# A gated cross-attention kernel on one core: its opening in another order

## The chip, the core and the metric

The kernel runs on one core of a Trainium2 chip. A core has five engines that work beside each other and wait for each other through semaphores: TensorE (PE, matrix products, with its weight loads shown apart as PEld), VectorE (DVE), ScalarE (ACT), GpSimd (POOL) and SyncE (SP), which here only issues DMAs. Data lie in SBUF; TensorE writes into eight PSUM banks, which VectorE and ScalarE read. The metric is the device time of one execution in microseconds (us), as the median of several runs.

## The reference

Two blocks, each with an attention over a context and a feed-forward part; a residual stream x of 4 x 512 x 128 goes through all four.

```
x = x + tanh(g_xattn[0]) * attention0(layernorm(x), ctx)     # 16 heads of 8, 154 keys
x = x + tanh(g_ffn[0])   * quantised_gated_ffn(layernorm(x)) # 128 -> 384 -> 128
x = x + tanh(g_xattn[1]) * attention1(layernorm(x), ctx)     # the same with a causal mask
x = x + tanh(g_ffn[1])   * scan_ffn(layernorm(x))            # a gated recurrence over the 4 elements
```

An attention is q = xn Wq' + bq, k = ctx Wk' + bk, v = ctx Wv' + bv, then softmax(q k' / sqrt(8)) v per head and a projection with Wo. Of the whole, the text that follows needs the first attention's opening: the layer norm of the batch elements, the keys, the queries and the maxima of the scores.

## The kernel before

The work is staged by batch element. The programs of the engines are written out by hand, each in its own order; `PE_PLAN`, `ACT_PLAN` and `DVE_PLAN` say at which slot of a step (i = -1 to 4, 20 slots each) a piece of an element's work stands. Each engine takes its instructions strictly in this order, so an instruction that waits holds all behind it.

The opening of the first layer runs thus:

- **Loads.** SyncE issues all loads in one go: x of element 0, the context, the key weights, three attention weights, the tail of the context, x of elements 1 to 3, then the weights of the later parts and the masks. ScalarE issues three small ones, `rows` among them.
- **Norm.** VectorE takes the statistics of an element (`norm_stats`, L1358 and L1361). GpSimd makes 1/sqrt(var + eps) (`root`, L641 and L643). Then the element is scaled to `xn`, by VectorE for the elements in `NORM_ON_DVE` (L1376) and by GpSimd for the others (L651 and L658). TensorE turns it into the one bank `misc` (`turn_normed`, L965) and ScalarE copies it to `xnT` (L759).
- **Keys.** Eight products (`keys`, L946) of 128 x 308: four groups of heads, each for elements 0 and 1 (part 0) and for 2 and 3 (part 1). ScalarE makes the high part `kh` of each (L728), VectorE the sum `K4` (L1309).
- **Query.** TensorE projects `xnT` into `misc` (`project_q`, L971), ScalarE writes its high part `qh` (L766), VectorE its low part `ql` from the same bank (L1416), and SyncE sends both by three DMAs into `Q4` (`queries`). `misc` has one user at a time, in the order of `misc_plan`.
- **Diagonal.** `K4` of one element is spread into the cleared tile `Kd` (L1699 and L746 for element 0, GpSimd's L536 for elements 2 and 3).
- **Units.** For element 0, 22 units: TensorE makes the scores of up to three heads for 128 queries into one of three banks (`scores_for_top`, L988), VectorE takes the maximum over the keys (`take_top`, L1425) and so frees the bank. Between the units TensorE has fillers (`fill`, L1121), whose results nobody reads. Behind unit 12 it turns the normed element 2, elsewhere it makes the values (L957) and the third query.
- **Behind it.** The maxima are split (L1436 and L1438), turned (L1002), copied (L778) and sent by DMAs (L462) into `Q4`; then the scores proper (L1020), exponentials (L787) and weighted values (L1052) of element 0 run, with the units of the next element between them.
- **GpSimd** has, beside the roots, a long list: clears of `Kd[0]` and `Q4[1]`; `Kd[1]`, `V4`, `VT` (L668 to L670); behind VectorE's diagonal copies `Q4[2]`, `Kd[2]`, `nil` (L505 to L507); norm of element 2; constants of V (L569 to L581); biases; values (L596 and L600); the low part of the third query; `KT` (L549); the diagonal of element 2 (L536).

## Time and profile before

| | |
|---|---|
| median of 3 runs | 335.45 us (334.67 to 335.69) |
| the profiled execution | 336.59 us, its span 334.6 us |
| TensorE busy | 294.6 us, 88% of the span |
| VectorE busy | 250.6 us, 75% |
| ScalarE busy | 190.9 us, 57% |
| GpSimd busy | 139.9 us, 42% |
| mean granted clock of TensorE | 0.974 of full |

A busy share is an average over the whole program. In the opening, each engine has its own gaps, and only the timelines of that stretch say which of them the next piece of work waits for. A timeline row gives the start of a group of like instructions, how long the group takes, the engine, the line, the operation, the tile written and the tiles read, the count, and in brackets how long the engine had stood idle and what ended that.

### The profile page before, as it was taken

To read this page: it belongs to the slowest core of one execution; us is meant where nothing else is said; L and a number is where in the kernel's file an instruction comes from. 1 tells how busy PE (TensorE), PEld (TensorE's weight loads), DVE (VectorE), ACT (ScalarE), POOL (GpSimd) and SP (SyncE) were. 2 spreads that over 40 slices of the span, in tenths; PEclk is the share of its full clock that TensorE was granted. 3 is DMA by queue.
4 is the path that set the end of the run, shared out by engine and by line. 5 is a ranking of instruction groups with operands and counts; after the bars stand their busy time and mean duration, and the time that the engine had idled before them with its cause. 6 is when DMAs were issued, how large, how long until landed. Compare 5 with 4: busy or idle time off the path is not lost. (4 is left out here: it accounts for less than half of the span.)

```text
span 334.6 us, 4564 instructions
## 1 busy us (share of the span) xinstructions
PE 294.6 (88%) x1456; PEld 169.4 (51%) x1456; DVE 250.6 (75%) x549; ACT 190.9 (57%) x311; POOL 139.9 (42%) x274
## 2 busy tenths in 40 slices
PE   1789899799989798996997879699989998999994
PEld 1458555455533364442545667574755654434462
DVE  5689877888987379999998895686697692442834
ACT  1672276466476744889899415236566557664232
POOL 6669892752050401684002194921386217141100
PEclk9979999999999999998999997879999999999999
DMA  7920100020000000000000102020002000000004
GB/s 214 357 98 34 71 31 11 0 102 10 1 8 3 0 0 2 1 0 1 0 0 2 69 25 95 2 102 0 10 6 101 4 2 9 0 3 0 1 2 125
DMA packets 9688, 12.57 MB, mean 38 GB/s; under 512 B 896, under 2 KB 5376, under 8 KB 9664
## 3 DMA queue, kind: packets, MB, share of 16 engines
q1 hardware_dynamic: 9232, 11.80, 9.9%
q10 hardware_dynamic: 432, 0.47, 0.7%
q8 instruction: 12, 0.20, 0.3%
q14 instruction: 12, 0.10, 0.1%
HBM read 4.27 MB, written 1.05 MB: 16 GB/s over the span
## 5 line engine op out<-in xcount | busy, mean ns | idle before, releaser
L1425 DVE TENSOR_REDUCE sb_nm<-ps_top 128x3 f32<-128x462 f32 (+2 forms) x168 | 97.7, 626 | 28.1 <-PE ps_top L988 17.9
L787 ACT ACTIVATE sb_pr<-ps_score 128x512 f32<-128x512 f32 (+1 forms) x148 | 81.9, 583 | 56.7 <-PE ps_score L1020 47.5
L988 PE MATMUL ps_top<-sb_Kd,sb_Q 128*128 128x462 f32 (+3 forms) x240 | 71.8, 355 | 4.1 <-DVE sb_nm L1425 3.2
L1020 PE MATMUL ps_score<-sb_Q,sb_Kd 128*128 128x512 f32 x119 | 54.7, 470 | 1.4 <-ACT sb_pr L787 1.0
L988 PEld LDWEIGHTS ps_top<-sb_Kd,sb_Q 128*128 128x128 f32 x240 | 45.1, 195 | 15.8 <-DVE sb_nm L1425 10.5
L1020 PEld LDWEIGHTS ps_score<-sb_Q,sb_Kd 128*128 128x128 f32 x119 | 22.2, 188 | 32.1 <-ACT sb_pr L787 26.7
L641 POOL TENSOR_SCALAR sb_var<-sb_mv 128x4 f32<-128x4 f32 x16 | 3.9, 242 | 75.6 <-DVE sb_mv L1361 75.1
L1052 PE MATMUL ps_pv<-sb_pr,sb_V 128*32 128x512 f32 x256 | 34.1, 605 | 0.0
L635 POOL TENSOR_SCALAR_AFFINE_SELECT sb_pr<-sb_pr 128x512 f32<-128x512 f32 x16 | 10.5, 659 | 43.9 <-ACT sb_pr L787 43.9
L1250 PE MATMUL ps_top<-sb_front,sb_wfT 128*128 128x512 f32 x44 | 22.0, 626 | 1.0 <-ACT sb_u L883 1.0
L643 POOL TENSOR_TENSOR sb_rstd<-sb_var,sb_half 128x4 f32<-128x4 f32 x16 | 19.4, 1211 | 1.3
L658 POOL TENSOR_SCALAR sb_xn<-sb_xr,sb_nmean,sb_rstd 128x128 f32<-128x128 f32 x44 | 19.2, 449 | 1.2
L1445 DVE STREAM_TRANSPOSE sb_oq<-ps_pv 128x512 f32<-128x512 f32 x16 | 10.8, 699 | 11.8 <-PE ps_pv L1052 11.6
L536 POOL CAST sb_Kd<-sb_K 32x616 fp32r<-32x616 f32 x20 | 14.0, 702 | 10.8 <-ACT sb_front L893 9.7
L1052 PE MATMUL ps_pv<-sb_pr,sb_VT 128*32 128x512 f32 (+1 forms) x128 | 14.9, 550 | 0.9 <-ACT sb_pr L787 0.9
L965 PE MATMUL ps_misc<-sb_consts,sb_xn 128*128 128x128 f32 x64 | 10.5, 288 | 6.0 <-POOL sb_xn L658 2.9
L1358 DVE BATCH_NORM_STATS2 sb_stat<-sb_xr 128x6 f32<-128x128 f32 x64 | 13.9, 279 | 1.1 <-DMA sb_xr<-x 0.9
L1250 PE MATMUL ps_score<-sb_front,sb_wfT 128*128 128x512 f32 x24 | 12.0, 618 | 3.0 <-DVE sb_amax L1532 3.0
L992 PE MATMUL ps_top<-sb_maskr,sb_identr 128*128 128x512 f32 (+3 forms) x48 | 14.0, 291 | 0.0
L1250 PEld LDWEIGHTS ps_top<-sb_front,sb_wfT 128*128 128x128 f32 x44 | 8.3, 202 | 10.5 <-issue 6.1
L619 POOL TENSOR_TENSOR sb_xg<-sb_xr,sb_bog 128x128 f32<-128x128 f32 x32 | 13.6, 455 | 0.1
L1026 PE MATMUL ps_score<-sb_Q,sb_KT 128*128 128x384 f32 (+1 forms) x29 | 12.7, 446 | 1.0 <-ACT sb_pr L787 1.0
(195 smaller groups left out, 556.7 us busy)
## 6 DMA issues: line engine op xcount, KB each, us to landing
sb_Q<-sb_qh SPq DMA_DIRECT2D x16, 256.0 KB, 2.4
sb_Q<-sb_ql SPq DMA_DIRECT2D x8, 256.0 KB, 3.3
sb_xr<-x SPq DMA_DIRECT2D x4, 256.0 KB, 7.2
out<-sb_xr SPq DMA_DIRECT2D x4, 256.0 KB, 2.5
sb_wsb<-w SPq DMA_DIRECT2D x1, 704.0 KB, 8.8
sb_wf<-wffn SPq DMA_DIRECT2D x1, 576.0 KB, 8.4
sb_wkr<-wkr SPq DMA_DIRECT2D x2, 256.0 KB, 6.4
sb_Q<-sb_nmT SPq DMA_DIRECT2D x16, 32.0 KB
```

The source lines that it names most:

```text
L536: ins = pool.tensor_copy(Kd[n % 3][q, :, j, :], K4[q, :, b, :])
L619: ins = pool.tensor_tensor(xg[:, n % 2, t, :], xr[:, TT * b + t, :], bog[:, layer, :], ALU.add)
L643: pool.tensor_tensor(rstd[:, k % 4, :], var[:, k % 4, :], half[:, :], ALU.pow).then_inc(rstd_r, 1)
L658: ins = pool.tensor_scalar(xn[:, kind == "post", t, :], xr[:, TT * b + t, :], nmean[:, k % 4, t:t + 1], rstd[:, k % 4, t:t + 1], ALU.add, ...
L787: act.activation(pr[:, k % PRING, q0:T], score_bank(B * layer + b, t)[:, q0:T], ACT.Exp, scale=SCALE).then_inc(exp_r, 1)
L988: ins = pe.matmul(cols[:, c0:c1, :], Q4[n % 3][:, g, P * qt:P * qt + P], Kd[n % 3][:, g, j:j + c1 - c0, 0:keys], start=True, stop=not mask ...
L992: ins = pe.matmul(cols[:, c0:c1, lo:keys], identr[:, :], maskM[:, 0:keys - lo].unsqueeze(1).to_broadcast([P, c1 - c0, keys - lo]), start=F ...
L1020: ins = pe.matmul(ps[:, :], Kd[n % 3][:, g, j, 0:P], Q4[n % 3][:, g, :], start=True, stop=True, skip_group_check=True)
L1052: ins = pe.matmul(acc[32 * g:32 * g + 32, q0:T], lhs, pr[:, (TILES * n + t) % PRING, q0:T], start=(r in (0, 2)), stop=(r >= 4), skip_group ...
L1250: pe.matmul(up_bank(t)[:, :], wfT[:, 3 * (t >= 12) + m, :], xq[:, c, :], start=True, stop=True).then_inc(fmm, 1)
L1358: ins = dve.bn_stats(stat6[:, k % 4, t, :], xr[:, TT * b + t, :])
L1425: dve.tensor_reduce(nm[:, :, :].rearrange("p t h -> p (t h)")[:, f0:f0 + heads], top[k % MRING][:, 0:keys * heads].rearrange("p (h k) -> p ...
```

## The change

- **Keys.** `KEY_ORDER` makes the four products for elements 0 and 1 first, those for elements 2 and 3 after them. The context is loaded in two halves, and only the second four wait for the second half. The first layer's keys use the banks score0, score1, pv0, top1, top2. Element 0's diagonal copies wait for four keys in place of eight.
- **First query** behind the third key on TensorE, its low part on VectorE behind the third key.
- **DMAs.** The first query's DMAs are issued behind six loads of SyncE's in place of twelve; tail, masks, x of elements 2 and 3 and `rows` come behind them, the weights of the later parts behind the third query.
- **Second element.** GpSimd norms it, ahead of its three clears. TensorE turns it behind unit 2 and projects its query behind unit 4; VectorE makes the low part in slot 4. The statistics of element 2 move from before the string of units to slot 4, as does the start of the fillers between units.
- **Fillers.** Twelve products on a tile of ones stand ahead of the first key, eight behind the last, in place of two on keys.

The order on TensorE from its first instruction to its second unit, before (L946 keys, L965 turn of an element, L971 query, L1127 fillers, L988 units):

```order
L946 MATMUL ps_score<-sb_ctx,sb_wkr 128x308 x2
L965 MATMUL ps_misc<-sb_consts,sb_xn 128x128 x4
L946 MATMUL ps_top<-sb_ctx,sb_wkr 128x308 x3
L971 MATMUL ps_misc<-sb_xnT,sb_wsb 128x512
L946 MATMUL ps_score<-sb_ctx,sb_wkr 128x308 x2
L946 MATMUL ps_top<-sb_ctx,sb_wkr 128x308
L965 MATMUL ps_misc<-sb_consts,sb_xn 128x128 x4
L1127 MATMUL ps_top<-sb_ctx,sb_wkr 128x308
L971 MATMUL ps_misc<-sb_xnT,sb_wsb 128x512
L1127 MATMUL ps_top<-sb_ctx,sb_wkr 128x308
L988 MATMUL ps_top<-sb_Kd,sb_Q 128x462
```

and now (L957 keys, L976 turn, L982 query, L1158 and L1170 fillers, L1001 units):

```order
L1158 MATMUL ps_top<-sb_ones 128x128 x12
L957 MATMUL ps_score<-sb_ctx,sb_wkr 128x308
L976 MATMUL ps_misc<-sb_consts,sb_xn 128x128 x4
L957 MATMUL ps_score<-sb_ctx,sb_wkr 128x308
L957 MATMUL ps_pv<-sb_ctx,sb_wkr 128x308
L982 MATMUL ps_misc<-sb_xnT,sb_wsb 128x512
L957 MATMUL ps_top<-sb_ctx,sb_wkr 128x308 x2
L957 MATMUL ps_score<-sb_ctx,sb_wkr 128x308 x2
L957 MATMUL ps_pv<-sb_ctx,sb_wkr 128x308
L1170 MATMUL ps_top<-sb_ones 128x128 x8
L1001 MATMUL ps_top<-sb_Kd,sb_Q 128x462
L1001 MATMUL ps_top<-sb_Kd,sb_Q 128x154
```

The second turn and the second query have left the stretch ahead of the first unit, and the first query has moved from behind five keys to behind three.

GpSimd from the root of the first element to the clears behind the diagonal copies, before (sb_V at L669 is V4, at L670 VT):

```order
L641 TENSOR_SCALAR sb_var<-sb_mv 128x4
L643 TENSOR_TENSOR sb_rstd<-sb_var,sb_half 128x4
L668 MEMSET sb_Kd 128x2464
L669 MEMSET sb_V 128x2048
L670 MEMSET sb_VT 128x1024
L641 TENSOR_SCALAR sb_var<-sb_mv 128x4
L643 TENSOR_TENSOR sb_rstd<-sb_var,sb_half 128x4
L505 MEMSET sb_Q 128x2048
L506 MEMSET sb_Kd 128x2464
L507 MEMSET sb_nil 32x512
```

and now:

```order
L648 TENSOR_SCALAR sb_var<-sb_mv 128x4
L650 TENSOR_TENSOR sb_rstd<-sb_var,sb_half 128x4
L648 TENSOR_SCALAR sb_var<-sb_mv 128x4
L650 TENSOR_TENSOR sb_rstd<-sb_var,sb_half 128x4
L658 TENSOR_SCALAR sb_nmean<-sb_mv 128x4
L665 TENSOR_SCALAR sb_xn<-sb_xr,sb_nmean,sb_rstd 128x128 x4
L676 MEMSET sb_Kd 128x2464
L677 MEMSET sb_V 128x2048
L678 MEMSET sb_VT 128x1024
L512 MEMSET sb_Q 128x2048
L513 MEMSET sb_Kd 128x2464
L514 MEMSET sb_nil 32x512
```

The second element's mean and scaling (L658 and L665) are new here, and stand ahead of the clears that were ahead of its root.

VectorE from the first keys to the statistics of element 2, before:

```order
L1309 SCALAR_TENSOR_TENSOR sb_K<-ps_score,sb_cols,sb_kh 128x308 x2
L1358 BN_STATS sb_stat<-sb_xr 128x6 x4
L1361 BN_AGGR sb_mv<-sb_stat 128x2 x4
L1309 SCALAR_TENSOR_TENSOR sb_K<-ps_top,sb_cols,sb_kh 128x308 x2
L1376 TENSOR_SCALAR sb_xn<-sb_xr,sb_mv,sb_rstd 128x128 x4
L1309 SCALAR_TENSOR_TENSOR sb_K<-ps_top,sb_cols,sb_kh 128x308
L1416 SCALAR_TENSOR_TENSOR sb_ql<-ps_misc,sb_cols,sb_qh 128x512
L1309 SCALAR_TENSOR_TENSOR sb_K<-ps_score,sb_cols,sb_kh 128x308 x2
L1309 SCALAR_TENSOR_TENSOR sb_K<-ps_top,sb_cols,sb_kh 128x308
L1699 CAST sb_Kd<-sb_K 32x4x154 x2
L1358 BN_STATS sb_stat<-sb_xr 128x6 x4
L1361 BN_AGGR sb_mv<-sb_stat 128x2 x4
```

and now:

```order
L1319 SCALAR_TENSOR_TENSOR sb_K<-ps_score,sb_cols,sb_kh 128x308 x2
L1368 BN_STATS sb_stat<-sb_xr 128x6 x4
L1371 BN_AGGR sb_mv<-sb_stat 128x2 x4
L1319 SCALAR_TENSOR_TENSOR sb_K<-ps_pv,sb_cols,sb_kh 128x308
L1426 SCALAR_TENSOR_TENSOR sb_ql<-ps_misc,sb_cols,sb_qh 128x512
L1319 SCALAR_TENSOR_TENSOR sb_K<-ps_top,sb_cols,sb_kh 128x308
L1705 CAST sb_Kd<-sb_K 32x4x154 x2
L1319 SCALAR_TENSOR_TENSOR sb_K<-ps_top,sb_cols,sb_kh 128x308
L1319 SCALAR_TENSOR_TENSOR sb_K<-ps_score,sb_cols,sb_kh 128x308 x2
L1319 SCALAR_TENSOR_TENSOR sb_K<-ps_pv,sb_cols,sb_kh 128x308
L1435 TENSOR_REDUCE sb_nm<-ps_top 128x3 x6
L1368 BN_STATS sb_stat<-sb_xr 128x6 x4
```

The scaling of the second element has left, the first query's low part stands two keys earlier, the diagonal casts stand ahead of four keys, and element 2's statistics stand behind six units.

The diff, cut to its core:

```diff
-SECOND_QLOW_AT = ((0, -1, 1), (1, -1, 7))
-FILL_FROM = (1, 3)
+SECOND_QLOW_AT = ((0, -1, 4), (1, -1, 7))
+FILL_FROM = (4, 3)
+KEY_ORDER = ((0, 2, 4, 6, 1, 3, 5, 7), tuple(range(8)))
...
-NORM_ON_DVE = {("pre", 0, 0), ("pre", 0, 1), ("post", 0, B - 1), ("pre", 1, 0), ("post", 1, B - 1)}
+NORM_ON_DVE = {("pre", 0, 0), ("post", 0, B - 1), ("pre", 1, 0), ("post", 1, B - 1)}
...
-        kbank = score + top
+        kbank = (score + pv[:1] + top[1:], score + top)
...
+        late_k_in = sem("late_k_in")
...
             sp.dma_start(xr[:, 0:TT, :], xd[:, 0]).then_inc(x_in[0], 16)
-            sp.dma_start(ctx_sb[:, :, :], ctxT).then_inc(k_in, 16)
             sp.dma_start(wkr_sb[:, 0, :, :], wkr[:, 0]).then_inc(k_in, 16)
+            sp.dma_start(ctx_sb[:, 0:2, :], ctxT[:, 0:2, :]).then_inc(k_in, 16)
             sp.dma_start(wsb[:, 0:WL1, :], w[:, 0:WL1, :]).then_inc(w_in, 16)
-            sp.dma_start(tail_sb[:, :, :], tailT).then_inc(tail_in, 16)
-            for b in range(1, B):
-                sp.dma_start(xr[:, TT * b:TT * b + TT, :], xd[:, b]).then_inc(x_in[b], 16)
-            sp.dma_start(wf_sb[:, :, :], wffn).then_inc(wf_in, 16)
-            sp.dma_start(wsb[:, WL1:NW, :], w[:, WL1:NW, :]).then_inc(wl_in, 16)
-            sp.dma_start(wkr_sb[:, 1, :, :], wkr[:, 1]).then_inc(wl_in, 16)
-            sp.dma_start(cmask[:, :], masks).then_inc(mask_in, 16)
+            sp.dma_start(xr[:, TT:2 * TT, :], xd[:, 1]).then_inc(x_in[1], 16)
+            sp.dma_start(ctx_sb[:, 2:B, :], ctxT[:, 2:B, :]).then_inc(late_k_in, 16)
...
-                for b in range(ahead(layer)):
-                    queries(layer, b)
+                queries(layer, 0)
+                if layer == 0:
+                    sp.dma_start(tail_sb[:, :, :], tailT).then_inc(tail_in, 16)
+                    sp.dma_start(cmask[:, :], masks).then_inc(mask_in, 16)
+                    sp.dma_start(xr[:, 2 * TT:3 * TT, :], xd[:, 2]).then_inc(x_in[2], 16)
+                    sp.dma_start(rows_sb[:, :, :], rows.partition_broadcast(P)).then_inc(rows_in, 16)
+                    sp.dma_start(xr[:, 3 * TT:4 * TT, :], xd[:, 3]).then_inc(x_in[3], 16)
+                queries(layer, 1)
...
+                    if (layer, i) == (0, -1):
+                        sp.dma_start(wf_sb[:, :, :], wffn).then_inc(wf_in, 16)
+                        sp.dma_start(wsb[:, WL1:NW, :], w[:, WL1:NW, :]).then_inc(wl_in, 16)
+                        sp.dma_start(wkr_sb[:, 1, :, :], wkr[:, 1]).then_inc(wl_in, 16)
...
                 normed("pre", layer, 0)
                 if layer == 0:
                     pool.wait_ge(xn_r, 1)
+                    normed("pre", 0, 1)
                     pool.memset(Kd[1][:, :, :, :].bitcast(F32), 0.0).then_inc(kd_clear, 1)
                     pool.memset(V4[:, :, :, :, :], 0.0).then_inc(zero_r, 1)
                     pool.memset(VT[:, :, :, :], 0.0).then_inc(zero_r, 1)
-                normed("pre", layer, 1)
+                if layer == 1:
+                    normed("pre", 1, 1)
...
-            act.dma_start(rows_sb[:, :, :], rows.partition_broadcast(P)).then_inc(rows_in, 16)
...
-                col = k // 2
+                col = G * layer + KEY_ORDER[layer][c] // 2
...
-                act.wait_ge(k4_r, 8 * layer + 8)
+                act.wait_ge(k4_r, 8 * layer + (8 if n > 0 else 4))
...
             copy_k(0, 0)
+            copy_normed("pre", 0, 0)
             copy_k(0, 1)
-            copy_normed("pre", 0, 0)
-            for c in (2, 3, 4):
+            copy_k(0, 2)
+            copy_q(0, 0)
+            for c in (3, 4, 5):
                 copy_k(0, c)
-            copy_q(0, 0)
-            for c in (5, 6, 7):
-                copy_k(0, c)
+            diagonal(0, 0)
+            copy_k(0, 6)
+            copy_k(0, 7)
             copy_normed("pre", 0, 1)
-            diagonal(0, 0)
             copy_q(0, 1)
             act.activation(identr[:, :], ident[:, :], ACT.Copy).then_inc(const_r, 1)
             act.wait_ge(mask_in, 16)
             act.activation(maskr[:, :], cmask[:, :], ACT.Copy).then_inc(const_r, 1)
+            diagonal(0, 1)
             act.wait_ge(rows_in, 16)
             act.activation(tg[:, :], rows_sb[:, RG, 0:4], ACT.Tanh).then_inc(gates, 1)
-            diagonal(0, 1)
...
-                part = c % 2
-                pe.matmul(kbank[c % ring][:, 0:2 * S], wkr_sb[:, layer, c // 2, :],
+                g, part = divmod(KEY_ORDER[layer][c], 2)
+                if layer == 0 and part == 1:
+                    pe.wait_ge(late_k_in, 16)
+                pe.matmul(kbank[layer][c % ring][:, 0:2 * S], wkr_sb[:, layer, g, :],
...
+                if k == MRING - 1:
+                    pe.wait_ge(k4_r, 5)
...
+            pe.wait_ge(ones_r, 1)
+            for _ in range(12):
+                pe.matmul(top[2][:, 0:P], ones[:, :], ones[:, :], start=True, stop=True, skip_group_check=True)
             pe.wait_ge(k_in, 32)
             keys(0, 0)
-            keys(0, 1)
             pe.wait_ge(small_in, 32)
             turn_normed("pre", 0, 0)
-            for c in (2, 3, 4):
+            for c in (1, 2):
                 keys(0, c)
             pe.wait_ge(w_in, 16)
             project_q(0, 0)
-            for c in (5, 6, 7):
+            for c in (3, 4, 5, 6, 7):
                 keys(0, c)
-            turn_normed("pre", 0, 1)
-            pe.wait_ge(k4_r, 5)
-            fill_with_keys(1)
-            project_q(0, 1)
-            fill_with_keys(1)
+            for _ in range(8):
+                pe.matmul(top[0][:, 0:P], ones[:, :], ones[:, :], start=True, stop=True, skip_group_check=True)
...
                             scores_for_top(layer, b, u)
+                            if (layer, i, b, u) == (0, -1, 0, 2):
+                                turn_normed("pre", 0, 1)
+                            if (layer, i, b, u) == (0, -1, 0, 4):
+                                project_q(0, 1)
...
-                g, part = divmod(c, 2)
+                g, part = divmod(KEY_ORDER[layer][c], 2)
...
             keys(0, 1)
             norm_stats("pre", 0, 1)
             keys(0, 2)
+            q_low(0, 0)
             keys(0, 3)
-            norm("pre", 0, 1)
-            keys(0, 4)
-            q_low(0, 0)
-            for c in (5, 6, 7):
-                keys(0, c)
             dve.wait_ge(kd_clear, 1)
-            dve.wait_ge(k4_r, 8)
+            dve.wait_ge(k4_r, 4)
             for j in (2, 3):
                 ins = dve.tensor_copy(Kd[0][32 * j:32 * j + 32, :, j, :], K4[32 * j:32 * j + 32, :, 0, :].bitcast(F32))
             ins.then_inc(kd0_r, 1)
+            for c in (4, 5, 6, 7):
...
-                        if (layer, i, slot) == (0, -1, 0):
+                        if (layer, i, slot) == (0, -1, 4):
                             norm_stats("pre", layer, 2)
```

## Rows read from the trace of the kernel before

**Rows 1.** The timeline of TensorE, 0 to 45 us.

```profile
7.30 2.42 PE L946 MATMUL ps_score<-sb_ctx,sb_wkr 128*128 128x308 f32 x4 [7.30 <-DMA sb_wkr<-wkr]
...
16.66 0.81 PE L965 MATMUL ps_misc<-sb_consts,sb_xn 128*128 128x128 f32 x4 [2.26 <-DVE sb_ql L1416]
...
18.29 2.01 PE L971 MATMUL ps_misc<-sb_xnT,sb_wsb 128*128 128x512 f32 x2
...
20.52 0.60 PE L988 MATMUL ps_top<-sb_Kd,sb_Q 128*128 128x462 f32 x1
...
28.64 0.60 PE L965 MATMUL ps_misc<-sb_consts,sb_xn 128*128 128x128 f32 x4
...
40.04 0.50 PE L1020 MATMUL ps_score<-sb_Q,sb_Kd 128*128 128x512 f32 x1
```

**Rows 2.** The timeline of VectorE, 0 to 50 us.

```profile
6.85 1.12 DVE L1376 TENSOR_SCALAR sb_xn<-sb_xr,sb_mv,sb_rstd 128x128 f32<-128x128 f32 x4 [1.39 <-POOL sb_rstd L643]
...
10.86 0.86 DVE L1358 BATCH_NORM_STATS2 sb_stat<-sb_xr 128x6 f32<-128x128 f32 x4
11.75 0.38 DVE L1361 BATCH_NORM_AGGREGATE sb_mv<-sb_stat 128x2 f32<-128x6 f32 x4
...
15.77 0.74 DVE L1416 SCALAR_TENSOR_TENSOR sb_ql<-ps_misc,sb_cols,sb_qh 128x512 fp32r<-128x512 f32 x1
16.42 0.98 DVE L1309 SCALAR_TENSOR_TENSOR sb_K<-ps_score,sb_cols,sb_kh 128x308 fp32r<-128x308 f32 x2
...
17.95 0.96 DVE L1699 CAST sb_Kd<-sb_K 32x616 fp32r<-32x616 f32 x2
...
21.17 0.64 DVE L1425 TENSOR_REDUCE sb_nm<-ps_top 128x3 f32<-128x462 f32 x1 [0.93 <-PE ps_top L988]
...
28.02 4.70 DVE L1425 TENSOR_REDUCE sb_nm<-ps_top 128x3 f32<-128x462 f32 x8 [0.20 <-PE ps_top L988]
33.10 1.95 DVE L1425 TENSOR_REDUCE sb_nm<-ps_top 128x3 f32<-128x462 f32 x4 [0.38 <-PE ps_top L988]
```

**Rows 3.** The timeline of GpSimd, 0 to 50 us.

```profile
8.03 2.15 POOL L668 MEMSET sb_Kd<- 128x2464 f32 x1 [1.28 <-DVE sb_xn L1376]
...
11.86 0.95 POOL L670 MEMSET sb_VT<- 128x1024 f32 x1
...
18.97 1.80 POOL L505 MEMSET sb_Q<- 128x2048 f32 x1 [4.78 <-DVE sb_Kd L1699]
...
23.41 0.19 POOL L641 TENSOR_SCALAR sb_var<-sb_mv 128x4 f32<-128x4 f32 x1
...
25.09 1.75 POOL L658 TENSOR_SCALAR sb_xn<-sb_xr,sb_nmean,sb_rstd 128x128 f32<-128x128 f32 x4
...
36.93 5.08 POOL L600 TENSOR_TENSOR sb_VT<-sb_tmp,sb_bvt 32x32 f32<-32x32 f32 x16
```

**Rows 4.** The timeline of ScalarE, 0 to 50 us.

```profile
10.46 0.60 ACT L759 ACTIVATE sb_xnT<-ps_misc 128x512 f32<-128x512 f32 x1
...
12.88 0.69 ACT L766 ACTIVATE sb_qh<-ps_misc,sb_cols 128x512 fp32r<-128x512 f32 x1 [0.25 <-PE ps_misc L971]
13.47 1.10 ACT L728 ACTIVATE sb_kh<-ps_score,sb_lcols,sb_consts 128x308 fp32r<-128x308 f32 x2
...
18.00 1.43 ACT L746 ACTIVATE sb_Kd<-sb_K 32x616 fp32r<-32x616 f32 x2
```

**Rows 5.** The timeline of the DMAs that SyncE issues.

```profile
37.06 1.29 SPq L462 DMA_DIRECT2D sb_Q<-sb_nmT  x2
```

**Rows 6.** A window: busy us (and instructions) per engine, PEclk, DMA share, GB/s.

```profile
17.00:20.00 3.00, 3.00 (x7) 1.44 (x6) 2.82 (x10) 1.91 (x3) 1.03 (x1) 0.50 0.24 92
```

**Rows 7.** The timeline of TensorE, 44 to 85 us.

```profile
44.72 1.07 PE L1052 MATMUL ps_pv<-sb_pr,sb_V 128*32 128x512 f32 x8
...
56.42 0.47 PE L1020 MATMUL ps_score<-sb_Q,sb_Kd 128*128 128x512 f32 x1
```

**Rows 8.** DMA issues: engine, count, KB each, median us from issue to landing.

```profile
sb_wsb<-w SPq DMA_DIRECT2D x1, 704.0 KB, 8.8
```

13 lines of the change are left out of this document (5 added, 8 removed).

## The prediction, made before the changed kernel ran

> **What bounds the kernel now.** I read the order of the instructions first, then the timelines of the engines over the first 50 us, then the waits, since the change touches nothing behind the opening. The opening has three parts. In the first, the loads, the keys and the first query are made. TensorE starts at 7.30, when the key weights have landed [rows 1]. VectorE has written the normed first element by 7.97 [rows 2]. The second part is a string of 22 "units": TensorE computes scores of up to three heads, VectorE takes their maxima. VectorE starts it at 21.17 and ends it at 35.05 [rows 2]. A full unit costs it 4.70 / 8 = 0.587 us, and it hardly pauses: this part is VectorE's. The last twelve maxima are the groups that start at 28.02 and 33.10, so unit 13 (counted from 0) starts at 28.02 + 3 x 0.587 = 29.78. The third part starts with the first scores at 40.04 [rows 1], 5.0 us behind the last maximum (the maxima are turned and sent through a DMA). From there TensorE is busy nearly without a gap, and what lies behind moves as a block if its start moves, unless another engine holds it.
>
> Before the first unit stands the second query. TensorE waits until 16.66 to turn it, since the one misc bank is still read by VectorE for the first query; from 17 to 20 it then runs at half its clock [rows 6], so that this query's projection takes 2.01 us from 18.29, and the first unit comes at 20.52 [rows 1]. VectorE had its share of the diagonal copies (Kd) done at 18.91 [rows 2], ScalarE its own at 18.00 + 1.43 = 19.43 [rows 4], so the second query cost the first unit about a microsecond.
>
> GpSimd is the second chain. It waits until 18.97, clears three tiles until 23.33, and norms the third element by 26.84: 3.43 us from 23.41 [rows 3]. TensorE turns that element behind unit 12, at 28.64, so it waits for nothing there [rows 1]. GpSimd goes on without a pause and has the values ready at 36.93 + 5.08 = 42.01 [rows 3]; TensorE uses them at 44.72 [rows 7], a slack of 2.71.
>
> **The opening, step by step.** The normed first element stays at 7.97: its load is first on its queue in both kernels, and nothing ahead of it is removed. The keys' loads come earlier (154 KB less of context, and the rows load moved away), but TensorE needs them by 8.0 only, so an earlier landing is worth nothing by itself. Then:
> - TensorE turns the element at 8.05; four transposes take 0.60 at full clock [rows 1]; ScalarE copies it in 0.60, to 9.25, then two key copies at 1.10 / 2, to 10.35 [rows 4]. VectorE writes key 1 at about 10.35 (0.98 / 2 each) [rows 2].
> - VectorE's statistics of the second element take 11.75 + 0.38 - 10.86 = 1.27 [rows 2], so they are ready at about 11.65. They were ready at 12.13.
> - The first query: projection behind two more keys, done at about 10.45; ScalarE's copy 0.69 [rows 4] gives 11.2; VectorE: key 2 to 12.15, low part 0.74 to 12.85, key 3 to 13.35, two diagonal casts 0.96 to 14.3, keys 4 and 5 to 15.3. ScalarE's diagonal copies (1.43) [rows 4] run from 13.35 to 14.8 and hold its last two keys, so VectorE ends key 7 at about 16.45. The query's DMAs issue at 12.9; the DMA of the maxima took from 37.06 to the scores that need it at 40.04, 3.0 us [rows 5, 1], so this one is there by 15.9. The eight fillers on TensorE end at about 14.8.
> - So VectorE's first maximum starts at 16.45 in place of 21.17: 4.7 us earlier. This is the gross gain.
>
> **What of it is paid back inside the string.** VectorE now has the third element's statistics (1.27) and the second query's low part (0.74, which it had before too) within the string. From 16.45, thirteen units cost 13 x 0.587 = 7.64, with 1.27 and 0.7 it is done with unit 12 at 26.05. The wait for the mask copies in front of unit 6 falls beside the statistics, and the second query's turn and projection stand beside maxima of units already made: both cost nothing while VectorE has two units ahead of it; without that cover they would cost half of 2.01 and 0.6.
>
> Now TensorE wants to turn the third element. It issues unit 12 once unit 9 is read, at 24.3, and is at the turn at 24.7. GpSimd has not normed it by then. In the changed kernel GpSimd norms the second element itself, before its clears: from 11.65, 3.43 us by the same four steps [rows 3] to 15.1. Then the three clears that ran from 8.03 to 11.86 + 0.95 = 12.81, 4.78 in all, hidden before in an idle stretch that ended at 18.97, now end at 19.9. Then the three that took 18.97 to 23.41, 4.44, to 24.3, and the third element, 3.43, to 27.8. GpSimd is therefore 0.95 us later than before (26.84), and TensorE, which is 3.9 us earlier, waits from 24.7 to 27.8. All that is queued behind the turn waits with it: unit 13, which VectorE needs at 26.05 and gets at about 28.45. Its string goes on from there as it did from 29.78: the net gain is 1.33.
>
> **The clock.** A stand of TensorE costs more than itself: behind its 2.26 us of idleness that ended at 16.66 the granted clock was 0.50, which is 1.2 in place of 2.4 GHz [rows 1, 6]. The new idle stretch is 3.1 us. At half clock a unit with its filler would still about keep up with 0.587, but the turn, the tail values (eight matmuls of 128 columns) and the third query's projection (2.01 against half of it) fall there; of it I count 0.6 on VectorE's string if the clock falls, and nothing if it does not. I take half: 0.3. Against this the twelve matmuls on ones ahead of the keys make the keys start warm; that is inside the steps above.
>
> **Behind the opening.** GpSimd's values come at 42.01 + 0.95 = 42.96; TensorE wants them at 44.72 - 1.0 = 43.7. No stall, but this slack caps the whole gain at 2.71 - 0.95 = 1.76. Late loads: w, wf and the second key weights are issued behind the third query, at about 45 (GpSimd's low part), beside a DMA system that otherwise idles. They are needed far later.
>
> **Sum.** 1.33 - 0.3 = 1.0 us off the profiled execution: 336.59 to 335.6; the median of the runs shown lies 1.14 below that execution, so 335.45 becomes 334.4. The bounds of the unknown parts: the clock 0 to 0.6; the wait for GpSimd, by the nearest rows, between none (2.3 more) and 1 us more than reckoned.
>
> **A rule that speaks against it.** VectorE's diagonal casts of 616 numbers took 0.96 / 2 = 0.48 us each while GpSimd stood idle [rows 2, 3]; in the new order they stand at 13.35 to 14.3, beside GpSimd's norming of the second element (11.7 to 15.1), and in the trace of before no such cast runs beside it. If one held the other up, GpSimd's chain would be up to 0.96 later. The Trainium skill, "SBUF — State Buffer", section "Who interferes with whom", says that a VectorE copy or cast in a two-port mode and a GpSimd instruction exclude each other for a whole instruction; by that rule the gain would be 0.96 smaller. No row of before decides it.
>
> **Rivals.**
> 1. *The gain is eaten* (GpSimd up to 0.96 later by the collision just named, or the full 0.6 of the clock, or both). GpSimd at 28.8, unit 13 at 29.4: gain 0.4, less the clock: -0.2 to 0.4. Time 335.3. For it: GpSimd's chain is now the one that decides, and each delay on it counts in full. Against: the casts may not meet an instruction of GpSimd's for their whole length.
> 2. *GpSimd is not late*: TensorE's turn finds the element there, or the statistics come a microsecond sooner. The gain is then the cap of the values, 2.7 at most, some 2.2: 333.2. Against it: the six clears and two normings add up to 16.1 us from 11.65, all from rows, with no gap to save.
> 3. *The other side, slower*: the late loads meet the DMA of the second maxima. That DMA takes 3.0 us and its scores stand at 56.42 [rows 7]; after it is issued at about 52 it has 0.4 us to spare. The loads are issued by 49 (1.5 MB). If they land as slowly as at the start, 8.8 us behind their issue for w [rows 8], they occupy the queues until 54.7, and the maxima land at about 57 in place of 55: a stall of some 1.6, which turns 1.0 of gain into 0.6 of loss: 336.1. It decides from a backlog beyond 52.4. Against it: at the start 4 MB stood in the queues, here 1.5.
> 4. *It does not do what it says*: the first unit stays at 20 since the query's DMA is late behind loads. Then the gain is below 0.5. The tail, mask and x loads are issued behind it, so I give it little and put it with the first.
>
> **Chances.** The forecast (gain 0.5 to 1.6) 0.52; gain eaten 0.23; GpSimd not late 0.15; slower 0.10. About 0.3%, 1.0 us, is what a measurement of this kernel can tell from no change. Half of the forecast's share and all of the second rival's lie beyond it: 0.43 faster. Half of the forecast, and the first rival, within it: 0.46. Slower: 0.11 with the tail of the first. The range leaves out the far ends on both sides, 333.0 to 336.1; the forecast's own range is 333.8 to 335.0.
>
> **What would show it.** VectorE's first maximum at 16 to 17; GpSimd's third element done at 27.5 to 28.5; a wait of TensorE's turn for GpSimd of about 3 us near 25, a half clock behind it or not; the last maximum of the string near 34; the first scores near 39; no wait for the values at 43. If TensorE does not wait at the turn, the second rival holds; if the scores of the second element wait for the maxima's DMA near 55, the third. A first maximum later than 18.5 would mean that the opening's steps are wrong.

## The result, and the profile after

| | before | changed |
|---|---|---|
| median, us (lowest to highest, 5 runs each) | 335.45 (334.67 to 335.71) | 337.39 (336.75 to 338.04) |
| ratio, 95% interval | | 1.0069 [1.0044, 1.0093] |
| the profiled execution: time, span, us | 336.59, 334.6 | 336.75, 334.7 |
| first scores of the first element, us from the start | 40.04 [rows 1] | 42.86 |

The change makes the kernel slower by 1.9 us, where 1.0 us faster was forecast. The two profiled executions are nearly equal in length (334.6 and 334.7), so the loss must be found by its landmarks, the times at which the same instruction starts in both, and not by their ends. Here and below, medians are of all runs, while the ratios leave out the runs of the kernel before that lay more than 1.5% above its fastest.

VectorE of the changed kernel. (Columns as before: start, busy us, engine, line, operation, tiles, count, [idle before it <- what ended that].)

```profile
16.65 3.50 DVE L1435 TENSOR_REDUCE sb_nm<-ps_top 128x3 f32<-128x462 f32 x6
...
22.99 2.81 DVE L1435 TENSOR_REDUCE sb_nm<-ps_top 128x3 f32<-128x462 f32 x5
30.30 1.92 DVE L1435 TENSOR_REDUCE sb_nm<-ps_top 128x3 f32<-128x462 f32 x3 [4.50 <-PE ps_top L1001]
33.89 1.32 DVE L1435 TENSOR_REDUCE sb_nm<-ps_top 128x3 f32<-128x462 f32 x2 [1.67 <-PE ps_top L1001]
35.90 1.95 DVE L1435 TENSOR_REDUCE sb_nm<-ps_top 128x3 f32<-128x462 f32 x4 [0.69 <-PE ps_top L1001]
```

The first maximum comes 4.52 us earlier than in [rows 2]. The first thirteen maxima run without a gap that the view shows. Then VectorE stands for 4.50, 1.67 and 0.69 us, each time for TensorE. The string, which [rows 2] ended at 35.05, ends at 37.85.

GpSimd, from the norm of the second element to the values:

```profile
12.19 0.19 POOL L648 TENSOR_SCALAR sb_var<-sb_mv 128x4 f32<-128x4 f32 x1 [5.10 <-DVE sb_mv L1371]
...
13.87 2.21 POOL L665 TENSOR_SCALAR sb_xn<-sb_xr,sb_nmean,sb_rstd 128x128 f32<-128x128 f32 x4
16.02 2.15 POOL L676 MEMSET sb_Kd<- 128x2464 f32 x1
...
20.75 1.80 POOL L512 MEMSET sb_Q<- 128x2048 f32 x1
...
26.89 1.74 POOL L665 TENSOR_SCALAR sb_xn<-sb_xr,sb_nmean,sb_rstd 128x128 f32<-128x128 f32 x4
...
38.73 5.08 POOL L607 TENSOR_TENSOR sb_VT<-sb_tmp,sb_bvt 32x32 f32<-32x32 f32 x16
```

It hardly pauses from 12.19 on, and still the third element is normed at 26.89 + 1.74 = 28.63, 1.8 us later than before (26.84). The four scaling instructions of the second norm took 2.21 us, of the third 1.74.

TensorE, at the places that the prediction named:

```profile
16.57 0.60 PE L976 MATMUL ps_misc<-sb_consts,sb_xn 128*128 128x128 f32 x4
...
20.53 0.48 PE L1001 MATMUL ps_top<-sb_Kd,sb_Q 128*128 128x308 f32 x2 [1.06 <-ACT sb_maskr L821]
...
28.68 1.11 PE L976 MATMUL ps_misc<-sb_consts,sb_xn 128*128 128x128 f32 x4 [3.87 <-POOL sb_xn L665]
...
31.55 1.91 PE L968 MATMUL ps_pv<-sb_wsb,sb_tail 128*128 128x128 f32 x8
...
42.86 0.50 PE L1033 MATMUL ps_score<-sb_Q,sb_Kd 128*128 128x512 f32 x1
...
47.54 1.07 PE L1065 MATMUL ps_pv<-sb_pr,sb_V 128*32 128x512 f32 x8
```

TensorE has no idle time ahead of the turn of the second element at 16.57 (2.26 in [rows 1]). Instead it stands for 3.87 us ahead of the third one. That turn takes 1.11 instead of the 0.60 of [rows 1]. The first scores are 2.82 us later than in [rows 1]; the values, ready at 43.81, are used at 47.54 without a wait.

Windows of the same kernel (columns: window, its length, busy us and instructions of PE, PEld, DVE, ACT, POOL, the granted clock, DMA share, GB/s):

```profile
24.00:28.00 4.00, 0.81 (x4) 0.30 (x2) 1.79 (x4) 0.09 (x1) 3.64 (x8) 0.98 0.18 70
28.00:30.00 2.00, 1.32 (x6) 1.33 (x7) 0.00 (x0) 0.17 (x1) 2.00 (x3) 0.50 0.00 0
30.00:35.00 5.00, 5.00 (x21) 4.71 (x21) 2.95 (x5) 1.03 (x2) 4.28 (x25) 0.53 0.00 0
35.00:40.00 5.00, 3.97 (x25) 3.00 (x23) 3.33 (x8) 1.85 (x3) 4.53 (x21) 1.00 0.00 2
```

Behind the stand the clock is at 0.50, 1.2 instead of 2.4 GHz, from 27.9 to 34.7. TensorE is then busy for 5.00 of 5.00 us while VectorE, which [rows 2] show busy nearly without a pause in the string, has work for 2.95: for this stretch the bound has moved from VectorE to TensorE.

**Why the two profiled executions end together.** The lateness of the first scores is carried nearly whole to GpSimd's norm root (the TENSOR_TENSOR that writes rstd) at 204.27, which stands at 201.64 before. Behind it both kernels have a wait of 2.62 us. First the kernel before, then the changed one, TensorE behind that wait:

```profile
215.83 1.03 PE L1002 MATMUL ps_misc<-sb_consts,sb_nms 128*32 128x128 f32 x4 [2.62 <-DVE sb_nms L1438]
...
217.51 0.63 PE L988 MATMUL ps_top<-sb_Kd,sb_Q 128*128 128x512 f32 x1
```

```profile
217.28 0.61 PE L1015 MATMUL ps_misc<-sb_consts,sb_nms 128*32 128x128 f32 x4 [2.62 <-DVE sb_nms L1448]
...
218.20 0.40 PE L1001 MATMUL ps_top<-sb_Kd,sb_Q 128*128 128x512 f32 x1
```

The same wait was followed by half clock in the one execution and not in the other. The next root stands at 242.33 and 242.38. So the changed kernel regains 2.6 us here. Of it 1.2 us lie ahead of the wait (from the root to this turn 14.19 us before and 13.01 now; the execution of before ran at half clock from 201.3 to 204.7 too, the changed one did not), and 1.4 us behind it. The work is the same in both kernels; what differs is the clock, so I put the 2.6 us down to these two executions and not to the kernels.

### The profile page after: what moved, and what is told of

Read it like the earlier page. It is cut to its first block and busy times, and to the rows that moved or that the text cites. A ratio compares the mean times of both kernels' runs of the same rounds, so it can differ in the third digit from the quotient of the medians.

```text
span 334.7 us, 4632 instructions
## 1 busy us (share of the span) xinstructions
PE 294.3 (88%) x1487; PEld 171.1 (51%) x1487; DVE 249.0 (74%) x545; ACT 191.1 (57%) x311; POOL 142.3 (43%) x279
## 5 line engine op out<-in xcount | busy, mean ns | idle before, releaser
L1001 PE MATMUL ps_top<-sb_Kd,sb_Q 128*128 128x462 f32 (+3 forms) x240 | 70.8, 351 | 4.9 <-DVE sb_nm L1435 2.8
L1001 PEld LDWEIGHTS ps_top<-sb_Kd,sb_Q 128*128 128x128 f32 x240 | 44.6, 194 | 16.8 <-DVE sb_nm L1435 10.8
L665 POOL TENSOR_SCALAR sb_xn<-sb_xr,sb_nmean,sb_rstd 128x128 f32<-128x128 f32 x48 | 21.4, 459 | 1.3
L1260 PE MATMUL ps_top<-sb_front,sb_wfT 128*128 128x512 f32 x44 | 20.8, 600 | 1.0 <-ACT sb_u L892 1.0
L976 PE MATMUL ps_misc<-sb_consts,sb_xn 128*128 128x128 f32 x64 | 10.5, 288 | 9.9 <-POOL sb_xn L665 6.7
L976 PEld LDWEIGHTS ps_misc<-sb_consts,sb_xn 128*128 128x128 f32 x64 | 7.3, 145 | 13.4 <-POOL sb_xn L665 9.1
L767 ACT ACTIVATE sb_xnT<-ps_misc 128x512 f32<-128x512 f32 x8 | 4.8, 596 | 16.2 <-PE ps_misc L976 16.2
```

The source lines that it names most:

```text
L665: ins = pool.tensor_scalar(xn[:, kind == "post", t, :], xr[:, TT * b + t, :], nmean[:, k % 4, t:t + 1], rstd[:, k % 4, t:t + 1], ALU.add, ...
L976: ins = pe.transpose(misc[:, P * t:P * t + P], xn[:, kind == "post", t, :], ident[:, :])
L1001: ins = pe.matmul(cols[:, c0:c1, :], Q4[n % 3][:, g, P * qt:P * qt + P], Kd[n % 3][:, g, j:j + c1 - c0, 0:keys], start=True, stop=not mask ...
L1260: pe.matmul(up_bank(t)[:, :], wfT[:, 3 * (t >= 12) + m, :], xq[:, c, :], start=True, stop=True).then_inc(fmm, 1)
```

## The experiments

The explanations tested were: the late third norm, with the stand and the half clock behind it, is the loss; the half clock is a small part of it, as the prediction priced it; the late loads are the loss (theory B). The experiments of the later comparisons ask in addition whether VectorE and GpSimd hold each other up, and whether the intended gain can be had. Ratios are to the kernel before, on the same chip and in the same comparison, with a 95% interval. "Root" is the landmark near 201 us just named. The landmarks come from one profiled execution of each kernel, whose time stands beside them, and where the clock fell in it moves them.

| kernel | third turn, us | first scores | root | profiled | median (runs) | ratio |
|---|---|---|---|---|---|---|
| before | 28.64 | 40.04 | 201.64 | 336.59 | 334.67 (29), 335.61 (35), 336.04 (20) | |
| changed | 28.68 | 42.86 | 204.27 | 336.75 | 337.39 (5) | 1.0069 [1.0044, 1.0093] |
| e1 | 24.84 | 36.09 | 205.03 | 337.90 | 336.90 (12) | 1.0064 [1.0029, 1.0099] |
| e2 | 28.30 | 39.53 | 201.00 | 335.99 | 335.92 (12) | 1.0049 [1.0016, 1.0082] |
| e3 | 28.91 | 40.14 | 201.56 | 334.52 | 337.89 (12) | 1.0051 [1.001, 1.0092] |
| e4 | 30.80 | 42.05 | 203.44 | 337.06 | 340.02 (6) | 1.0123 [1.0062, 1.0183] |
| e5 | 25.63 | 36.84 | 200.48 | 334.52 | 333.35 (12) | 0.9937 [0.991, 0.9964] |
| e6 | 28.33 | 41.27 | 205.44 | 339.53 | 337.44 (12) | 1.0069 [1.0035, 1.0102] |
| e7 | 28.23 | 39.58 | 201.04 | 335.23 | 334.94 (12) | 0.9972 [0.9938, 1.0006] |
| e8 | 29.84 | 42.64 | 203.97 | 336.56 | 338.99 (12) | 1.0088 [1.005, 1.0126] |
| e9 | 26.04 | 37.25 | 199.92 | 331.67 | 331.78 (10) | 0.9907 [0.9873, 0.9942] |
| e10 | 24.79 | 36.02 | 197.62 | 331.93 | 331.93 (9) | 0.99 [0.9856, 0.9943] |

e1 to e4, then e5 to e8, then e9 and e10 were compared together; the three medians of before belong to them in this order.

### e1: the third norm ahead of GpSimd's last clears

```diff
                 if layer == 0:
-                    clear_rest()
                     normed("pre", 0, 2)
+                    clear_rest()
                     frames()
```

> The changed kernel with one GpSimd piece moved: the norm of element 2 ahead of the three clears behind the diagonal copies (Q4[2], Kd[2], nil), not behind them. Theory A (TensorE stands at the turn of element 2 since GpSimd comes late, and the half clock that follows costs as much again): the normed element is ready near 24.8 in place of 28.6, TensorE's stand of 3.9 us goes, the clock stays full, the 22 units end near 32.3 in place of 37.85, the first scores come near 37.3 in place of 42.86. GpSimd's values then come at 44.3 and TensorE stands for them about 3 us in place of the gain: in all 2.5 to 3 us less than the changed kernel, about 335. Theory B (the moved loads or DMAs cost the time): stays at 337.4.

The stand at the third turn is gone and the first scores come 6.8 us earlier than in the changed kernel, but the time is no better: 336.90, where about 335 was expected. TensorE of e1:

```profile
24.84 0.66 PE L976 MATMUL ps_misc<-sb_consts,sb_xn 128*128 128x128 f32 x4
...
36.09 0.50 PE L1033 MATMUL ps_score<-sb_Q,sb_Kd 128*128 128x512 f32 x1
...
44.43 1.26 PE L1065 MATMUL ps_pv<-sb_pr,sb_V 128*32 128x512 f32 x8 [3.58 <-POOL sb_VT L607]
```

The sum of GpSimd's work is unchanged, so the values are ready at 44.38, and the wait has moved there: 3.58 us, with half clock from 45.2 to 48.6 behind it. The root, at 205.03, has lost the whole lead. Its way there also held two later half clocks (65.7 to 69, 157.8 to 164.6), so this run does not say how much of the loss is the wait alone. Moving one item within a full chain moves the wait; what has to change is what the chain holds.

### e2: fillers ahead of the third turn

```diff
                             if what in ("pre", "post"):
+                                if (what, layer, b) == ("pre", 0, 2):
+                                    fill(32)
                                 turn_normed(what, layer, b)
```

> The changed kernel with 32 more fillers on TensorE ahead of the turn of element 2, so that it is busy while GpSimd is late. Theory A with the clock: GpSimd's element still comes at 28.6, but the clock stays full and the last nine units take 5.3 us as in the kernel before, not 7.55: the string ends near 34.6, 3.2 us sooner, time 334.2 to 334.8. Theory C (the wait alone costs, the clock does nothing on a string that VectorE bounds, as the prediction had it): string end at 37, time 337. Theory B: 337.4.

The 32 filler matmuls write what TensorE's fillers of this stage always write. They leave the stand of the string as it is and take only TensorE's idleness away. TensorE, and then VectorE, of e2:

```profile
24.12 4.10 PE L1134 MATMUL ps_score<-sb_maskr,sb_identr 128*128 128x256 f32 x33
28.30 0.66 PE L976 MATMUL ps_misc<-sb_consts,sb_xn 128*128 128x128 f32 x4
...
39.53 0.50 PE L1033 MATMUL ps_score<-sb_Q,sb_Kd 128*128 128x512 f32 x1
```

```profile
29.25 1.73 DVE L1437 TENSOR_REDUCE sb_nm<-ps_top 128x3 f32<-128x462 f32 x3 [3.87 <-PE ps_top L1001]
31.17 1.19 DVE L1437 TENSOR_REDUCE sb_nm<-ps_top 128x3 f32<-128x462 f32 x2 [0.18 <-PE ps_top L1001]
32.73 1.96 DVE L1437 TENSOR_REDUCE sb_nm<-ps_top 128x3 f32<-128x462 f32 x4 [0.38 <-PE ps_top L1001]
```

VectorE's later gaps shrink from 1.67 and 0.69 to 0.18 and 0.38, and the last nine maxima take 5.44 us (29.25 to 34.69) where the changed kernel needed 7.55 (30.30 to 37.85). The first scores are 3.33 us earlier, of which 0.38 is the earlier turn: 2.95 us are the clock's. At this landmark the expectation that the clock costs much more than 0.6 us is borne out.

The medians do not show it. That of e2 is 1.25 above that of before, where 0.5 less to 0.1 more was expected, and its interval overlaps that of the changed kernel. A part of the puzzle is the yardstick: the profiled execution of before ran at half clock from 17 to 20.4, while e7, whose opening holds the same instructions, did not, and has its first scores at 39.58 and its root at 201.04. Against these, e2 (39.53 and 201.00) is level and not ahead. Why its median is still 1.25 higher stays open.

### e6: the changed kernel once more

> The changed kernel itself once more, for a comparison on the same chip: 336.5 to 338, and the root near 204.3.

The loss repeats: 1.0069 again. The root does not come where it was expected, but at 205.44: the clock fell twice more on the way to it (66.0 to 69.4 and 158.2 to 165.0), which it did not in the first profile. In this execution the half clock behind the stand was half as long (28.5 to 31.9), with the turn at 28.33 as in e2. The first scores at 41.27 lie 1.74 behind those of e2, and 1.24 ahead of the changed kernel's once the turn's 0.35 is taken off. So, from three executions, 3.4 us at half clock cost 1.7 us in this string, and 6.8 us cost 2.95.

### e7: the kernel before, with only the late loads of the change

```diff
-            sp.dma_start(wf_sb[:, :, :], wffn).then_inc(wf_in, 16)
-            sp.dma_start(wsb[:, WL1:NW, :], w[:, WL1:NW, :]).then_inc(wl_in, 16)
-            sp.dma_start(wkr_sb[:, 1, :, :], wkr[:, 1]).then_inc(wl_in, 16)
...
                         queries(layer, 2)
+                    if (layer, i) == (0, -1):
+                        sp.dma_start(wf_sb[:, :, :], wffn).then_inc(wf_in, 16)
+                        sp.dma_start(wsb[:, WL1:NW, :], w[:, WL1:NW, :]).then_inc(wl_in, 16)
+                        sp.dma_start(wkr_sb[:, 1, :, :], wkr[:, 1]).then_inc(wl_in, 16)
```

> The kernel before with one part alone: wf, w and the second key weights are loaded behind the third query. Theory A: within 0.5 us of the kernel before, the root within 0.3 of 201.64. Theory B (these loads collide with the maxima's DMA or the queries): 1 us or more later.

0.9972 [0.9938, 1.0006]: the loads do no harm that this measurement can tell. The root stands at 201.04, 0.6 earlier than in the kernel before and not within 0.3 as expected: the first scores are 0.46 earlier already, in an opening without half clock (see e2). In the changed kernel w and wf landed 5.1 and 4.1 us behind their issue, where w took 8.8 in [rows 8].

```profile
sb_wsb<-w SPq DMA_DIRECT2D x1, 704.0 KB, 5.1
sb_wf<-wffn SPq DMA_DIRECT2D x1, 576.0 KB, 4.1
```

### e8: the changed kernel without its twelve products on ones

```diff
-            for _ in range(12):
-                pe.matmul(top[2][:, 0:P], ones[:, :], ones[:, :], start=True, stop=True, skip_group_check=True)
```

> The changed kernel without the twelve products on ones ahead of the first key. Theory A: the first query comes about 1 us later at half clock, VectorE's first maximum at 17 to 17.5 in place of 16.65, GpSimd's chain 0.3 later at most, so the stand at the third turn is the same 3.9 us and the end within 0.5 us of the changed kernel.

TensorE's opening takes nearly twice as long for each instruction: two key matmuls 1.24 instead of 0.68, the query's projection 1.91 instead of 1.02. The first maximum comes at 18.73 instead of 16.65, more than expected. GpSimd's chain starts 1.07 us later (13.26 for 12.19), where 0.3 at most was expected, so the third turn comes at 29.84, behind a shorter stand (2.79 instead of 3.87). The first scores, at 42.64, seem unmoved, but only since the half clock behind the stand lasted 3.4 us here (30.5 to 33.9) and 6.8 us in the changed kernel's profile. Beside e6, whose half clock was as short, the turn is 1.51 us later and the first scores are 1.37 later. The median is 1.55 above that of e6, in the same comparison, with intervals that overlap. So by the traces the twelve products are worth about 1.4 us at the first scores, where the expectation kept the end within 0.5: they bring GpSimd's statistics forward too.

### e4: the kernel before, with GpSimd's new order

```diff
-NORM_ON_DVE = {("pre", 0, 0), ("pre", 0, 1), ("post", 0, B - 1), ("pre", 1, 0), ("post", 1, B - 1)}
+NORM_ON_DVE = {("pre", 0, 0), ("post", 0, B - 1), ("pre", 1, 0), ("post", 1, B - 1)}
...
                     pool.wait_ge(xn_r, 1)
+                    normed("pre", 0, 1)
                     pool.memset(Kd[1][:, :, :, :].bitcast(F32), 0.0).then_inc(kd_clear, 1)
```

> The kernel before with one part of the change alone: GpSimd norms the second element, ahead of its three clears. Theory A: GpSimd's third norm comes at about 28.5 in place of 26.84, which is when TensorE turns it in this kernel (28.64), so the time stays within 0.5 us of the kernel before: the later norm costs only where TensorE comes earlier. If the GpSimd order is dear by itself (a collision of GpSimd and VectorE throughout): over 336.5.

This missed by 5 us (340.02, against 334.67 for the kernel before), and led to the second mechanism. VectorE's diagonal casts (0.96 us in [rows 2]), then GpSimd's clears at the same time:

```profile
18.59 3.92 DVE L1701 CAST sb_Kd<-sb_K 32x616 fp32r<-32x616 f32 x2
```

```profile
16.90 2.15 POOL L669 MEMSET sb_Kd<- 128x2464 f32 x1
18.99 1.80 POOL L670 MEMSET sb_V<- 128x2048 f32 x1
20.73 0.95 POOL L671 MEMSET sb_VT<- 128x1024 f32 x1
```

The two casts end at 22.51, behind the last clear (21.68). The first of them alone took 3.43 us: it started at 18.59, beside the first clear, and was held over the two clears that started after it as well. Nothing was added to VectorE; it was held up for 2.96 us, and TensorE's first unit with it (2.34 us of idleness ahead of 22.66).

### e3: the second norm back on VectorE, the rest as changed

```diff
-NORM_ON_DVE = {("pre", 0, 0), ("post", 0, B - 1), ("pre", 1, 0), ("post", 1, B - 1)}
+NORM_ON_DVE = {("pre", 0, 0), ("pre", 0, 1), ("post", 0, B - 1), ("pre", 1, 0), ("post", 1, B - 1)}
...
                     pool.wait_ge(xn_r, 1)
-                    normed("pre", 0, 1)
...
-                if layer == 1:
-                    normed("pre", 1, 1)
+                normed("pre", layer, 1)
...
                 keys(0, c)
+            norm("pre", 0, 1)
```

> The changed kernel with the second element normed by VectorE (behind its eighth key) and GpSimd in the order of before. Theory A: VectorE's first maximum comes 1.1 us later (17.8), GpSimd's third norm is ready near 26, no stand of more than 0.5 us, values near 41.3, string end near 33.2, first scores near 38.2: 1.8 us ahead of the kernel before, so 333.5 to 334. Theory B: 337 or more.

The time misses the expectation by some 4 us, and the first scores come at 40.14, no earlier than before. The twelve runs fall into two groups, four at 334.5 to 334.8 and eight at 337.8 to 339.3, and the profiled one is of the first; what the others had more is in no trace. The norm on VectorE is the place, shown below with its counterpart.

### e9: e3, with a wait of GpSimd ahead of its clears

```diff
             def clear_rest():
                 pool.wait_ge(kd0_r, 1)
+                pool.wait_ge(xn_r, 2)
```

> e3 (the second element normed by VectorE behind its eighth key) with one wait more: GpSimd's three clears behind the diagonal copies begin only when that norm is written. In e3 the four instructions of the norm took 2.67 us at 16.73, beside GpSimd's clears of Q4[2] and Kd[2]; in the kernel before they took 1.12. Theory E (a VectorE instruction of this kind and a GpSimd clear exclude each other for a whole instruction): 1.12 us again, VectorE's first maximum near 17.9 in place of 19.33, the third turn near 26.5 to 27.5 in place of 28.9. Rival (the loads that land from 14 to 20 us, or a wait, stretch the norm): 2.67 us stays.

The norm on VectorE and the clear beside it in e3, first VectorE and then GpSimd:

```profile
16.73 2.67 DVE L1384 TENSOR_SCALAR sb_xn<-sb_xr,sb_mv,sb_rstd 128x128 f32<-128x128 f32 x4
19.33 2.82 DVE L1433 TENSOR_REDUCE sb_nm<-ps_top 128x3 f32<-128x462 f32 x5
```

```profile
16.50 2.15 POOL L513 MEMSET sb_Kd<- 128x2464 f32 x1
```

And in e9, where the clears begin behind the norm:

```profile
16.66 1.11 DVE L1385 TENSOR_SCALAR sb_xn<-sb_xr,sb_mv,sb_rstd 128x128 f32<-128x128 f32 x4
17.68 2.81 DVE L1434 TENSOR_REDUCE sb_nm<-ps_top 128x3 f32<-128x462 f32 x5
```

```profile
17.89 1.81 POOL L513 MEMSET sb_Q<- 128x2048 f32 x1 [3.22 <-DVE sb_xn L1385]
```

The same four instructions take 2.67 us beside the clears and 1.11 alone. In e3 TensorE stood 2.69 us for them (its turn came at 19.46), and half clock followed. One added wait moved the ratio from 1.0051 to 0.9907, since it makes GpSimd idle where it has time. The loads land in e9 as in e3, so the rival falls, and the exclusion is shown by taking it away.

### e5 and e10: other contents for GpSimd's chain

e5:

```diff
-                    normed("pre", 0, 1)
                     pool.memset(Kd[1][:, :, :, :].bitcast(F32), 0.0).then_inc(kd_clear, 1)
-                    pool.memset(V4[:, :, :, :, :], 0.0).then_inc(zero_r, 1)
                     pool.memset(VT[:, :, :, :], 0.0).then_inc(zero_r, 1)
+                    normed("pre", 0, 1)
+                    pool.memset(V4[:, :, :, :, :], 0.0).then_inc(zero_r, 1)
```

> The changed kernel with two of GpSimd's three clears (Kd[1] and VT, 2.15 + 0.95 us) ahead of the norm of the second element, in the stretch from 7.1 to 12.2 us in which GpSimd is idle; V4 stays behind it. Theory A (GpSimd's chain decides, and TensorE's stand brings the half clock): the third norm is ready near 25.5 in place of 28.6, TensorE stands 0.7 us in place of 3.9, the clock stays full, the string ends near 32 in place of 37.85, the first scores come near 37, the values near 40.8, ahead of TensorE. The same root of the norm at 201.64 in the kernel before comes 2.5 to 3 us sooner than there, at about 199; time 332 to 333. Theory D (GpSimd's clears and VectorE's copies hold each other up wherever they meet, so that clears ahead of the norm cost VectorE as much): less than 1 us is won.

e10, where VectorE clears VT at its start:

```diff
-                    normed("pre", 0, 1)
                     pool.memset(Kd[1][:, :, :, :].bitcast(F32), 0.0).then_inc(kd_clear, 1)
                     pool.memset(V4[:, :, :, :, :], 0.0).then_inc(zero_r, 1)
-                    pool.memset(VT[:, :, :, :], 0.0).then_inc(zero_r, 1)
+                    normed("pre", 0, 1)
...
             dve.memset(Q4[0][:, :, :].bitcast(F32), 0.0).then_inc(q4_clear, 1)
+            dve.memset(VT[:, :, :, :], 0.0).then_inc(zero_r, 1)
```

> The changed kernel with GpSimd's chain cut further: Kd[1] and V4 are cleared in its idle stretch ahead of the second norm, VT by VectorE while it waits for x. Theory A: the third norm waits for its statistics only and is ready near 24.8, TensorE does not stand at the third turn, the string ends near 31.3, the first scores come near 36.2, the values near 40.1 with TensorE at 40.8. About 0.7 us better than e5: 332.5 to 333. If the gain of e5 is limited elsewhere: no better than e5, 333.3.

Both put clears where the changed kernel's GpSimd waits for the second element's statistics (5.10 us idle ahead of 12.19, above). In e5 the stand at the third turn is 0.89 us and no half clock follows it. Its first scores (36.84) and values (40.73) come as expected; the root, at 200.48, is 1.5 later than expected and the median 0.35 above the range. Half clocks from 37.2 to 40.6 and from 153.2 to 160 lie on the way, which no run explains: the first is not there in e10, and is in e9. In e10 TensorE does not stand at the third turn. TensorE of e10:

```profile
24.79 0.66 PE L975 MATMUL ps_misc<-sb_consts,sb_xn 128*128 128x128 f32 x4
...
36.02 0.50 PE L1032 MATMUL ps_score<-sb_Q,sb_Kd 128*128 128x512 f32 x1
...
40.70 0.64 PE L1064 MATMUL ps_pv<-sb_pr,sb_V 128*32 128x512 f32 x4
```

The string ends at 31.18, the values are ready at 39.9, ahead of their use, and the whole 4.02 us at the first scores are still there at the root. e10 and e9 are the fastest, 1.0% and 0.9% below before, and both beat the changed kernel.

## Why the prediction was wrong

**Right.** The opening's steps: first maximum forecast at 16.45, measured at 16.65; turn of the second element and its projection (16.57, 18.20) and the wait for the mask copies ahead of unit 6 beside other work. TensorE stands at the third turn for GpSimd: forecast 3.1 us, measured 3.87. The values' slack holds, and the late loads cost nothing in e7. The third rival, that they delay the second maxima's DMA, is refuted in the changed kernel itself: that DMA is issued at 55.65 and its scores stand 3.42 us behind it, as in the kernel before (53.00 and 56.42). The rival that the query's DMA comes late did not happen either: the first unit waits 0.41 us for it, to 15.77.

**The step that failed is the clock.** The prediction gave it "0.6 on VectorE's string if the clock falls", and entered 0.3. It fell in both profiles of the changed kernel, and cost 2.95 us in the one and 1.7 in the other, measured against e2. The prediction held that at half clock "a unit with its filler would still about keep up with 0.587", and that only the turn, the tail values and the third query's projection cost, 0.6 in all. TensorE behind the stand at half clock, in the changed kernel (the turn at 28.68 and the tail values at 31.55 are shown above):

```profile
29.44 0.82 PE L1001 MATMUL ps_top<-sb_Kd,sb_Q 128*128 128x154 f32 x2
...
33.12 0.73 PE L1001 MATMUL ps_top<-sb_Kd,sb_Q 128*128 128x462 f32 x1
...
34.54 1.10 PE L982 MATMUL ps_misc<-sb_xnT,sb_wsb 128*128 128x512 f32 x2
35.08 0.78 PE L1001 MATMUL ps_top<-sb_Kd,sb_Q 128*128 128x308 f32 x2
```

And at full clock, in e2 (the turn at 28.30):

```profile
28.72 0.50 PE L1001 MATMUL ps_top<-sb_Kd,sb_Q 128*128 128x154 f32 x2
...
29.87 1.05 PE L968 MATMUL ps_pv<-sb_wsb,sb_tail 128*128 128x128 f32 x8
30.68 0.45 PE L1001 MATMUL ps_top<-sb_Kd,sb_Q 128*128 128x462 f32 x1
...
31.46 1.02 PE L982 MATMUL ps_misc<-sb_xnT,sb_wsb 128*128 128x512 f32 x2
31.91 0.78 PE L1001 MATMUL ps_top<-sb_Kd,sb_Q 128*128 128x308 f32 x2
```

From start to start:

| TensorE, us | changed | e2 | more |
|---|---|---|---|
| turn | 0.76 | 0.42 | 0.34 |
| three units with fillers | 2.11 | 1.15 | 0.96 |
| tail values | 1.57 | 0.81 | 0.76 |
| two units with fillers | 1.42 | 0.78 | 0.64 |
| third query's projection | 0.54 | 0.45 | 0.09 |
| in all | 6.40 | 3.61 | 2.79 |

A unit with its filler takes 3.53 / 5 = 0.71 us at half clock, more than VectorE's 0.587, so the units do not keep up: they make 1.60 of the 2.79. The three pieces that the prediction named make 1.19, twice its 0.6. And nothing is hidden: VectorE cannot draw on units already made, since it used them up during the stand. A stand thus removes its own cover.

**A term too small: GpSimd's lateness.** Forecast 0.95 us, measured 1.79 (28.63 against 26.84). Of the missing 0.84, 0.46 is the scaling of the second norm, 2.21 instead of 1.75, beside VectorE's two casts at 13.66; the statistics came 0.38 later than reckoned (12.03 for 11.65), 0.35 of it since the first element's load landed later in this execution (VectorE's first statistics start at 4.42 and not at 4.07). The prediction named the collision in its first rival and bounded it by 0.96; place and direction were right.

**The sum at the first scores.** Forecast 40.04 - 1.0 = 39.04, measured 42.86, a miss of 3.82. The clock cost 2.95 where 0.3 was entered, 2.65 more; GpSimd's 0.84 makes 3.49; 0.33 is left. Most of that is the step from the third element to unit 13: the forecast has its maximum 28.45 - 27.8 = 0.65 behind the normed element, in e2 it stands 29.25 - 28.30 = 0.95 behind the turn. The row that the sum starts from, 40.04, was itself of an execution with half clock in its opening; in e7 it is 39.58.

In the chances, half of the forecast's share and all of the second rival's are 0.41, not 0.43.

The gain itself is real: e10, with neither stand nor half clock, has its first scores 4.02 ahead of before. The stand gives 3.51 of it back (e10 to e2), the clock 2.95 more, the later turn 0.38:

| | first scores, us | step |
|---|---|---|
| e10: no stand, full clock | 36.02 | |
| e2: stand, full clock | 39.53 | +3.51 |
| e6: stand, 3.4 us at half clock | 41.27 | +1.74 |
| changed: stand, 6.8 us at half clock | 42.86 | +1.59, of it 0.35 the turn |

**The profile's time and the median.** The prediction took the 1.14 us between them as a constant. The changed kernel's profiled execution came at 336.75, only 1.15 above the forecast of 335.6 for it, and its median is 0.64 above that, where the median of before was 1.14 below. Two executions differ by where the clock falls, so the ends of two profiles do not carry a finding. That the changed kernel is slower, and that e5, e9 and e10 are faster, rests on the medians; how the loss divides into stand and clock rests on the landmarks of one execution each.
